# Transposing the next group's first half one product earlier, in the last attention phase of a four-layer graph network

## The reference, cut to what matters

```python
h = jnp.maximum(_layernorm(x, axis=-1), 0.0)
q, k, v = split_heads(h @ Wq + bq), split_heads(h @ Wk + bk), split_heads(h @ Wv + bv)
scores = einsum('bhqd,bhkd->bhqk', q, k) / sqrt(32) + beta * adj[:, None]
scores = where(adj[:, None] > 0, scores, -9e15)
out = einsum('bhqk,bhkd->bhqd', softmax(scores), v)
x = x + out          # heads put back side by side
```

## Time and profile before

| | us |
|---|---|
| median of 3 runs | 2679.72 (2678.27 to 2680.42) |
| the profiled execution, its own time | 2678.51 |
| its span, first to last instruction | 2676.8 |
| TensorE busy in the span | 2641.2 (99%) |
| VectorE, ScalarE, GpSimd busy | 1775.0, 1238.2, 1070.7 |
| mean granted TensorE clock | 0.997 of full |

### The profile page before, as it was taken

How to read it: one execution, slowest core, us unless ns; L and a number is a source line. 1 busy time by engine, 2 the same in 40 slices (tenths; PEclk the granted TensorE clock), 3 DMA queues, 4 the chain that set the end, 5 groups by cost and what they waited for, 6 DMA issues and landing times.

```text
span 2676.8 us, 78128 instructions
## 1 busy us (share of the span) xinstructions
PE 2641.2 (99%) x31118; PEld 2313.9 (86%) x31118; DVE 1775.0 (66%) x4030; ACT 1238.2 (46%) x2175; POOL 1070.7 (40%) x1092
## 2 busy tenths in 40 slices
PE   7999999999999999999999999999999999999998
PEld 6889888887888888888888888888888888998897
DVE  6777777775455554545577777777777786666665
ACT  4444444454454444444453433343343345565564
POOL 2434344442322422432333434444444444455454
PEclk9999999999999999999999999999999999999999
DMA  4222212225112212212221112112112112322221
GB/s 146 76 74 64 69 57 72 74 72 162 47 46 83 77 31 70 81 36 60 76 56 59 42 45 71 41 39 76 41 39 76 40 65 86 96 79 84 88 89 62
DMA packets 187155, 183.93 MB, mean 69 GB/s; under 512 B 79632, under 2 KB 186896, under 8 KB 187024
## 3 DMA queue, kind: packets, MB, share of 16 engines
q1 hardware_dynamic: 187024, 181.99, 22.3%
HBM read 131.61 MB, written 50.33 MB: 68 GB/s over the span
## 4 chain that ended last, share of the span: by engine, by line
PE 95%; DVE 2%; issue 1%; SPq 1%; POOL 0%; DMA 0%; ACT 0%; DVEq 0%; ACTq 0%; POOLq 0%
PE banks L59 70%; PE banks L924 4%; PE banks L2604 3%; PE banks L912 3%; PE banks L905 3%; PE banks L1787 2%; PE banks L2517 2%; PE banks L2538 2%; PE banks L1811 2%; PE banks L882 2%; PE banks L1743 1%; PE banks L933 1%; PE banks L2549 0%; DMA w_raw<-in_L_gnn_Wq 0%; DVE l_s_b L679 0%
## 5 line engine op out<-in xcount | busy, mean ns | idle before, releaser
L59 PE MATMUL banks<-w_hi,hT_hi 128*128 128x384 f32 x1152 | 401.4, 348 | 4.6 <-DVE l_left L2330 4.6
L59 PE MATMUL banks<-w_hi,hT_lo 128*128 128x384 f32 x1152 | 387.3, 336 | 0.0
L59 PE MATMUL banks<-w_lo,hT_hi 128*128 128x384 f32 x1152 | 386.5, 336 | 0.0
L59 PE MATMUL banks<-hT_hi,w_hi 128*128 128x512 f32 (+1 forms) x954 | 364.7, 382 | 1.3 <-DVE hT_lo L654 1.2
L59 PE MATMUL banks<-hT_hi,w_lo 128*128 128x512 f32 (+1 forms) x954 | 354.0, 371 | 0.0
L59 PE MATMUL banks<-hT_lo,w_hi 128*128 128x512 f32 (+1 forms) x954 | 353.8, 371 | 0.0
L1458 ACT ACTIVATE l_m<-banks 128x512 f32<-128x512 f32 x192 | 114.6, 599 | 396.5 <-PE banks L59 392.8
L343 POOL TENSOR_TENSOR l_s_d<-l_s_b,l_mx 128x768 f32<-128x768 f32 x128 | 188.3, 1476 | 254.2 <-DVE l_mx L684 250.5
L59 PE MATMUL banks<-w_hi,l_hT_hi 128*128 128x384 f32 x768 | 266.6, 347 | 3.8 <-DVE l_lin L1574 3.8
L59 PE MATMUL banks<-w_hi,l_hT_lo 128*128 128x384 f32 x768 | 258.9, 337 | 0.0
L59 PE MATMUL banks<-w_lo,l_hT_hi 128*128 128x384 f32 x768 | 258.8, 337 | 0.0
(11 more groups left out here) (231 smaller groups left out, 6032.9 us busy)
## 6 DMA issues: line engine op xcount, KB each, us to landing
after_l<-xr SPq DMA_DIRECT2D x160, 192.0 KB, 1.9
l_xl<-after_l SPq DMA_DIRECT2D x37, 768.0 KB, 5.0
xr<-after_l SPq DMA_DIRECT2D x24, 768.0 KB, 4.6
xr<-in_x SPq DMA_DIRECT2D x64, 192.0 KB, 2.4
xr<-after_l SPq DMA_DIRECT2D x64, 192.0 KB, 2.3
out_x<-xr SPq DMA_DIRECT2D x64, 192.0 KB, 2.1
xa<-in_x SPq DMA_DIRECT2D x15, 768.0 KB, 5.2
xa<-after_l SPq DMA_DIRECT2D x11, 768.0 KB, 7.0
```

Of the source, the lines that this page charges most:

```text
L59: last = nc.tensor.matmul(out, lhs[a](c), rhs[b](c), start=(m == 0), stop=(m == n - 1))
```

## The change

In the last phase, the transposes of tiles 0 and 1 of the next group leave the start of a turn and are written at the end of the turn before, behind the scores of tiles 0 and 1 and ahead of the value product of tile 1. The wait on `eT_set` (in the first turn on `hT_set`) that stood ahead of them goes. In the first turn they keep their place between the first scores and the value product of tile 2.

```diff
@@ plain_turn
         def plain_turn(i, opening, ahead, further):
             n = i + 1
             first_half, second_half = slice(0, 2 * P), slice(2 * P, COLS)
-            if ahead:
-                pe.wait_ge(hT_set if opening else eT_set, i * TILES + (TILES if opening else 0))
-                transposes(n, 0)
-                transposes(n, 1)
             pe.wait_ge(v_set, i * TILES + 1)
             values(i, 2)
@@
                 scores(n, 0)
                 scores(n, 1)
+                if further:
+                    transposes(n + 1, 0)
+                    transposes(n + 1, 1)
                 values(n, 1)
@@ ahead of the turns
             scores(0, 0)
             scores(0, 1)
+            transposes(1, 0)
+            transposes(1, 1)
             turns(pe, plain_turn)
```

## The result

The changed kernel takes 2686.89 us (median of 8 runs, 2686.48 to 2688.78) against 2679.76 us beside it (8 runs): 7.1 us more, ratio 1.0028, 95% interval 1.002 to 1.0037. It is slower by a small, real amount. 2688.1 was forecast. Two executions that stood beside these runs went at a lower granted clock and are left out of every median here: one of the kernel before, 8044.67 us at 0.307 of full, and one of the run with both repairs, 4700.90 us at 0.78.

What follows compares the result with a forecast made beforehand. It took TensorE's instruction list, 95% of the span, as the bound. A delay of 0.60 us in each of 14 turns, 8.4 us, on the median of 2679.7 gave 2688.1 us; range 2684.3 to 2691.5.

Steps and rivals of the forecast that it cites:

- Nobody waited for the transposes: Transposes of tiles 0 and 1: done sooner they start no one sooner, ScalarE being on vX; gain zero.
- The product ends 0.60 us later: values(n, 1), behind the six moved transposes, ends 3.31 us after the scores start instead of 2.71.
- twin: Turn 3's scores of two tiles, six transposes, then a value product; it priced the moved block at 0.63 us.
- Rival D: Product delayed by less than 0.60 us, or only place 1 holds: 0.36 us a turn, 5.0 us, 2684.7; chance 6%.
- Every link moves along: From vX(1) through hT_hi, hT_lo, maximum, biases and GpSimd to the exponentials, all move by 0.60 us.
- Place 1: exp_transposes(i, 0), waiting for ScalarE's exponential: slack 0.24 us, so TensorE will stand 0.36 us.
- Place 2: transposes(n, 2), waiting for add_bias of tile 3: slack 0, TensorE stands another 0.24 us.
- Place 3: exp_transposes(i, 1), waiting for exponentials(i, 1): slack 0, no further stand.
- TensorE's own list: TensorE's instructions up to values(i, 2): 0.02 us longer after the change, or nothing.
- Rival A: The chain has unseen slack at all three places, so the time stays, 2678.0 to 2679.7 us; chance 9%.
- C: Rows transposed sooner remove the stand at place 2: up to 4.2 us gained, 2675.5; gain over 0.2%: chance 2%.
- Rival B: A gap of 0.18 to 0.25 us comes with the block's new place each turn: 2690.6 to 2691.6 us; chance 10%.

Runs made afterwards that it cites:

- the run with both repairs: Changed kernel with the first hT_hi and hT_lo made ahead of vX(1), and maximum(i, 1) ahead of the second hT_lo; 2679.13 us, ratio 0.9999.
- the useless copy: Kernel before with a needless ScalarE copy between the vX copies of tile 1 and hT_hi, TensorE's list untouched; 2686.86 us, ratio 1.0028.

## Why the prediction was right, step by step

**Nobody waited for the transposes.** Right. Earlier transposes started nobody earlier; ScalarE took `hT_hi` up only behind vX, 0.02 to 0.03 us after it in both kernels.

**The product ends 0.60 us later.** Measured 0.61: 1.21 us from the scores' load to the block (2310.85 - 2309.64), 0.63 for the block, 1.48 for the product. The row chosen as a twin for the price of the block, with the same neighbours on both sides, gave it to 0.01 us. The 0.57 us of the block in its old place would have been a worse choice. So would the two estimates of its length, 0.34 and 0.49 us, that the prediction works out from the Trainium skill, "TensorE: Matmul & The Clock Gate", section "Back-to-back issue gap": the block of six takes 0.63 us in its new place too. Rival D did not come.

**Every link moves along.** Right, as the idle times show (0.61 more ahead of vX and ahead of `hT_lo`), and the useless copy shows it without any change on TensorE.

**The three places.** Place 1: slack 0.24 and a stand of 0.36 forecast, 0.44 measured, which makes exp_transposes(i, 0) come 0.38 later behind the scores of its turn. Place 2: 0.24 more forecast, 0.23 more measured. That its "issue" gap is the wait for the biases was read from the first turn; the two runs with the maximum ahead show it, since the gap goes when the biases come sooner. Place 3 had been given no further stand, and has none.

**What was mis-sized.** Two terms, both small and without effect on the sum. The first is TensorE's own list: the prediction has it 0.02 us longer, from the start of values(i, 2), and the stretch from scores to scores came out 0.06 shorter. values(i, 2) does start 0.03 us later (3.49 us behind the scores' load against 3.46). But now it follows another value product directly, and the step from its first matmul to its second is 0.17 us (2313.30 - 2313.13) where it was 0.26 (2310.39 - 2310.13), which the prediction left out. So TensorE comes to place 1 earlier and stands the longer there; the chain sets the turn, and the 0.06 us are not gained. The second is the slack of 0 at places 2 and 3. It is less than that: TensorE comes there late, for 0.12 us a turn. As these stands are in both kernels, the difference between the two doesn't feel them.

**The sum.** 14 x 0.60 = 8.4 us forecast; 14 x 0.61 = 8.5 in the traces; 7.1 and 8.9 in the medians. Rival A (hidden slack) is refuted by the copy in the chain, and C (a gain) by the result: `hT_hi` still waits for vX. Rival B (a gap with the block's new place) did not come: the block follows the scores after 1.21 us, as its twin does. The 0.02 us a turn between the run with both repairs and the kernel before with the maximum first isn't the 0.02 of the prediction: it is the small stand left at place 1, less the 0.04 us by which the stretch from scores to scores is shorter.

## What to carry to other kernels

An engine that is busy for 99% of the span can still have no time to spare against a chain on the other engines: before a block is put ahead of an instruction, look who starts at that instruction's end, follow the chain to where it comes back, and compare each link's end, plus the 0.12 us seen here between a releaser's end and the weight load, with the arrival there. To start a block earlier pays only if its reader would start earlier; a reader whose strictly ordered list holds another job first won't. And where an unnamed gap repeats, look for a turn in which the suspected releaser is early: if the gap is gone there, it is likely a wait. Reordering the releaser's list (here the maximum ahead of two copies) tests it, and may win a part of the gap back: here 0.12 us a turn.

## What the runs showed that was not expected

The last turn of the phase can have a stand at a place where TensorE's list has no wait and the profile names none. The twelve transposes of exponentials in it ran in one piece in the kernel before, and in two with a gap in the second execution of the changed kernel, whose first profile didn't have it. The weight loads, of before and of that execution:

```profile
2667.69 1.29 PEld L912 LDWEIGHTS banks<-ident,l_e_x 128*128 128x128 f32 x12
```

```profile
2676.68 0.86 PEld L912 LDWEIGHTS banks<-ident,l_e_x 128*128 128x128 f32 x8
2678.50 0.47 PEld L912 LDWEIGHTS banks<-ident,l_e_x 128*128 128x128 f32 x4 [0.97 <-issue]
```

The gap lies in the middle of tile 3's six transposes, and both tiles' exponentials had ended by 2676.93, 1.5 us before it closed. The same came with 0.97 us where the first parts are made early and with 1.24 us where both repairs were made; in the kernel before with the maximum first a gap of 1.61 us (1.48 between the matmuls, at the border of tiles 2 and 3) ends 2.1 us behind the last exponential. The phase's first scores moved between 2217.3 and 2221.8 us over these profiles as well, with the same instructions of TensorE ahead of them. The cause of either wasn't tried. Both are of the size by which single times here scatter, and the length of a turn, which neither touches, was the better measure.
